# Embedding of a language-model tower on one Trainium2 core: half of the hidden tiles finished by TensorE and ScalarE, and the next stage's first rows loaded one batch earlier

## What is computed

```python
freq, phase, amp = frequencies[ids], phases[ids], amplitudes[ids]          # 64 each
theta = 2 * pi * freq * t[None, :, None] + phase
wave = concatenate([amp * sin(theta), amp * cos(theta)], axis=-1)          # 128 wide
h = einsum('btf,df->btd', wave, W_proj) + b_proj + token_bias[ids]         # 512 wide
h = h + attn(layernorm(h))          # attention reads the normalised rows
h = h + ffn(layernorm(h))           # routed experts and a shared one
```

## Time and profile before

| what | value |
|---|---|
| median of three runs | 3596.42 us |
| the profiled execution's own time | 3624.72 us |
| its span | 3622.9 us |
| embedding, from the start of the span to attention's first matmul | 260.9 us |
| mean granted TensorE clock over the span | 0.943 of full speed |
| busy: PE, DVE, POOL, ACT | 3221.6, 2086.9, 1753.1, 1218.9 us |

### The profile page before, as it was taken

One profiled execution on the slowest core, in us unless ns is written; L12 is line 12 of the kernel. 1 busy time (PEld: TensorE's weight loads), 2 busy tenths in 40 slices (PEclk: granted clock), 3 DMA queues, 4 the chain that ended last, 5 costly groups with the idle time before them and its releaser, 6 DMA issues. The chain is left out here.

```text
span 3622.9 us, 61678 instructions
## 1 busy us (share of the span) xinstructions
PE 3221.6 (89%) x20358; PEld 1667.9 (46%) x20366; DVE 2086.9 (58%) x5798; ACT 1218.9 (34%) x2823; POOL 1753.1 (48%) x988
## 2 busy tenths in 40 slices
PE   4667999989999999999999899999999998687998
PEld 2334444444444444444444444444444444255775
DVE  6843444466646664666466645664566466755555
ACT  3661333333333333333233323332333233311111
POOL 5740354455545553555355535553555355643322
PEclk8878999999999999999999999999999998888999
DMA  5862200121111001010101010101010100205996
GB/s 186 302 255 74 91 30 4 45 73 53 57 69 48 18 16 54 16 36 14 56 16 36 13 54 19 36 13 54 19 36 13 53 19 13 73 4 172 258 254 149
DMA packets 121810, 253.64 MB, mean 70 GB/s; under 512 B 38749, under 2 KB 39389, under 8 KB 118929
## 3 DMA queue, kind: packets, MB, share of 16 engines
q1 hardware_dynamic: 77152, 200.36, 16.4%
q0 software_dynamic: 44048, 49.26, 5.3%
q10 hardware_dynamic: 288, 0.00, 0.0%
HBM read 144.61 MB, written 202.16 MB: 96 GB/s over the span
## 5 line engine op out<-in xcount | busy, mean ns | idle before, releaser
L967 POOL TENSOR_TENSOR a_first_probs<-a_first_probs,a_probs 128x2048 f32<-128x2048 f32 (+3 forms) x320 | 1031.5, 3224 | 1010.8 <-ACT a_probs L1047 928.4
L1205 DVE CUSTOM_DVE_ANT_0 a_unused<-a_ps_ring,a_work 128x512 bf16<-128x512 f32 (+3 forms) x1536 | 779.0, 555 | 897.9 <-PE a_ps_ring L1535 894.0
L1047 ACT ACTIVATE a_probs<-a_ps_ring 128x512 f32<-128x512 f32 (+3 forms) x1280 | 508.2, 473 | 365.0 <-PE a_ps_ring L1569 256.0
L1559 PE MATMUL a_ps_ring<-a_k_t,a_q_t 32*128 32x512 f32 (+3 forms) x3072 | 436.7, 536 | 78.1 <-DVE a_row_max L1205 52.6
L1535 PE MATMUL a_ps_ring<-a_q_t,a_k_t 32*128 32x512 f32 (+3 forms) x3072 | 393.8, 552 | 14.5 <-DVE a_row_max L1205 12.5
L978 POOL DMA_INDIRECT d_slots<-a_rows,a_place_i x349 | 350.0, 1003 | 71.9 <-issue 61.2
L1559 PEld LDWEIGHTS a_ps_ring<-a_k_t,a_q_t 32*128 32x128 f32 x3072 | 156.4, 185 | 281.3 <-issue 130.4
L1535 PEld LDWEIGHTS a_ps_ring<-a_q_t,a_k_t 32*128 32x128 f32 x3072 | 145.2, 190 | 283.4 <-issue 257.4
L974 POOL TENSOR_TENSOR a_attn_t<-a_attn_t,a_sum_inv 128x512 f32<-128x512 f32 x64 | 83.2, 1301 | 379.8 <-DVE a_sum_inv L1220 379.8
L1047 ACT ACTIVATE a_first_probs<-a_ps_ring 128x512 f32<-128x512 f32 x256 | 135.8, 606 | 381.9 <-PE a_ps_ring L1569 356.9
L1582 PE MATMUL a_ps_heads<-a_probs,a_values 128*32 128x512 f32 (+3 forms) x2560 | 261.6, 481 | 0.0
(11 more groups left out here) (283 smaller groups left out, 4325.9 us busy)
## 6 DMA issues: line engine op xcount, KB each, us to landing
d_hidden<-e_hidden SPq DMA_DIRECT2D x8, 2048.0 KB
d_normed_t<-e_normed_t SPq DMA_DIRECT2D x8, 2048.0 KB, 11.8
a_work<-d_normed_t SPq DMA_DIRECT2D x7, 2048.0 KB
a_hidden<-d_hidden SPq DMA_DIRECT2D x56, 256.0 KB, 2.7
out<-a_hidden SPq DMA_DIRECT2D x56, 256.0 KB
d_slots<-a_rows SPq DMA_DIRECT2D x32, 408.8 KB, 5.9
x_rows<-d_slots SPq DMA_DIRECT2D x32, 408.8 KB
x_w_gate<-w_gate SPq DMA_DIRECT2D x16, 512.0 KB
```

The lines of the kernel that those rows point to most:

```text
L967: nc.gpsimd.tensor_tensor(total_of, total_of, probs_of(m)[:, :, 0:width], ALU.add).then_inc(added, 1)
L1047: nc.scalar.activation(probs_of(m)[:, h, 0:width], score_bank(m, h)[:, 0:width], ACT.Exp).then_inc(exp_done, 1)
L1205: nc.vector.tensor_tensor_reduce(unused[:, (HG * k + h) % N_UNUSED, 0:width], row_bank(k, h)[:, 0:width], decay[:, at:at + width], 1.0, NE ...
L1559: nc.tensor.matmul(score_bank(m, h)[:, 0:width], q_t[st.g][dims, j * P:(j + 1) * P], k_t[st.g][dims, i0:i0 + width], start=True, stop=False)
```

## The change

Tiles with odd t are treated in another way. TensorE adds their token bias rows itself, by a third matmul with the identity as weights and the gathered rows as moving operand (f32, 512 columns, L491 of the changed kernel), and ScalarE then moves the finished tile from PSUM to `hidden` (its own `take_hidden`, at L412, placed last in its step of tile t). It counts in a new semaphore `hidden_taken`. Even tiles stay with DVE as they were. Whoever waited for `hidden_done` now waits for the one of the two counters that belongs to the tile, or for both (POOL before it gathers over a buffer, SP before it loads into one).

The load of attention's first rows stands behind batch 5 in SP's order and no longer behind batch 6.

```diff
+        def by_act(t):
+            return t % 2 == 1
+        def wait_hidden(eng, n):
+            if n >= 0:
+                eng.wait_ge(hidden_taken if by_act(n % NT) else hidden_done, n // 2 + 1)
+        def wait_batches(eng, count):
+            eng.wait_ge(hidden_done, NT // 2 * count)
+            eng.wait_ge(hidden_taken, NT // 2 * count)
...
-                if b == NB - 2:
-                    sp.wait_ge(hidden_done, NT * (NB - 2))
+                if b == NB - 3:
+                    wait_batches(sp, NB - 2)
...
             def take_stats(b, t):
-                dve.wait_ge(hidden_done, NT * b + t + 1)
+                wait_hidden(dve, NT * b + t)
...
-                    take_hidden(b, t)
+                    if not by_act(t):
+                        take_hidden(b, t)
...
+            def take_hidden(b, t):
+                if t == 1:
+                    wait_from_1(act, hidden_out[b % 3], 16 * (b // 3))
+                act.wait_ge(hid_ps_full, NT * b + t + 1)
+                nc.scalar.activation(hidden[b % 3][:, t, :], ps_hid[(NT * b + t) % 3][:], ACT.Identity).then_inc(hidden_taken, 1)
...
                             take_turned(b - 1, t - 2)
+                    if b < NB and by_act(t):
+                        take_hidden(b, t)
...
-                wait_from_1(pe, hidden_done, n - 2)
+                wait_hidden(pe, n - 3)
                 nc.tensor.matmul(bank[:], ones_b[:], b_parts[:], start=True, stop=False)
-                nc.tensor.matmul(bank[:], waves_t[b % 2][:, t, :], w_proj[:], start=False, stop=True).then_inc(hid_ps_full, 1)
+                mm = nc.tensor.matmul(bank[:], waves_t[b % 2][:, t, :], w_proj[:], start=False, stop=not by_act(t))
+                if by_act(t):
+                    if t == 1:
+                        pe.wait_ge(rows_in[b % 3], 16 * NT * (b // 3 + 1))
+                    mm = nc.tensor.matmul(bank[:], ident[:], rows[b % 3][:, t, 3 * NF:NROW], start=False, stop=True)
+                mm.then_inc(hid_ps_full, 1)
```

More of the change, by code:

```diff
@@ L194, in embed @@
         normed_out = [sem(f"normed_out{p}") for p in range(2)]
+        hidden_taken = sem("hidden_taken")
         N_CONSTS = 4
         ANGLE_STEPS = 8
+        def by_act(t):
[6 more added lines that the diff above has]
+            eng.wait_ge(hidden_taken, NT // 2 * count)
         block = ctx.enter_context(nc.Block())
@@ L252, in _ @@
                 if 1 <= b < NB - 2:
-                    pool.wait_ge(hidden_done, NT * b)
+                    wait_batches(pool, b)
                 for t in range(NT):
```

## The result

The changed kernel takes **3611.32 us** (median of 7 runs, 3608.91 to 3613.00) against 3596.42 of the kernel before (7 runs): ratio 1.0037, 95% interval 1.0025 to 1.0049. It is 15 us (0.4%) slower. The forecast was 10.8 us faster, with a range of 3577 to 3597.

What follows compares the result with a forecast made beforehand. In the embedding's middle batches DVE was taken to bound the first half, ACT and PE the second. 10.4 + 1.9 - 3.0 + 1.5 = 10.8 us less, from 3596.4 to 3585.6 us, range 3577 to 3597.

Steps and rivals of the forecast that it cites:

- The 3362 us behind that keep their instructions: Behind the embedding: instructions stay the same, so attention's span was to be unchanged within 2 us.
- Middle batches, 10.4 us: Embedding batches 2 to 5: each gains 2.6 us, from a shorter DVE first half, 10.4 us in all.
- The walk: First half of a middle batch: DVE stepped between POOL's additions, reaching the take of tile 4 2.7 us earlier.
- the additions take the gain back: Rival, embedding batches: DVE arrives earlier but always behind an addition, gaining 0.4 us per batch; 3594.8 us, chance 0.15.
- Batches 0, 1, 6, 1.9 us: These embedding batches gain 0.7, 0.5 and 0.7 us, 1.9 us in sum, bounds 0 and 6.
- Batch 7, a loss of 3.0 us: Last embedding batch, bound by ACT: evictions in every second tile cost 3.0 us, bounds 2.0 and 5.
- the closed chain: Batch 7: eviction, centre, scale, transposes and three matmuls follow one another, 4.36 us per pair of tiles, not 3.41.
- The load, 1.5 us: Embedding's end: with the load behind batch 5, batch 7's stores finish sooner, gaining 1.5 us, bounds 0 and 5.2.
- ACT becomes the bound: Rival, embedding: slow PE delays ACT's sines, 1.1 us lost in each of seven batches; 3605.6 us, chance 0.09.
- a change in attention: Behind the embedding: listed as a sign that the forecast is wrong; attention's span was to stay within 2 us.

Runs made afterwards that it cites:

- after: The changed kernel as profiled, with odd tiles by TensorE and ScalarE and the earlier load, against the kernel before: 3611.32 us, ratio 1.0037.
- e5: The changed kernel plus 64 do-nothing semaphore increments at the end of TensorE's list in the embedding: 3591.24 us, ratio 0.9983.
- e2: The changed kernel without its load part, attention's first rows loaded behind batch 6 as before: 3621.01 us, ratio 1.0062.
- e6: The kernel before plus 128 do-nothing semaphore increments at the end of TensorE's list in the embedding: 3619.33 us, ratio 1.0062.
- e1: The kernel before, unchanged, measured and profiled once more: 3598.48 us, ratio 1.000.
- e7: The changed kernel without POOL's additions of attention's output bias in the embedding, POOL only counting: 3585.06 us.
- e8: The kernel before without POOL's additions of attention's output bias in the embedding, POOL only counting: 3570.58 us.
- e13: The changed kernel with 64 increments, POOL's additions moved behind its gathers and out of DVE's first half: 3579.47 us, ratio 0.9943.
- e14: The kernel before with POOL's additions moved behind its gathers and out of DVE's first half: 3580.20 us, ratio 0.9947.
- e3: The kernel before with only the load of attention's first rows moved behind batch 5: 3597.48 us, ratio 1.0002.
- e15: The kernel of e13 with seven of each batch's eight POOL additions also waiting for DVE's last multiplication of the waves: 3574.59 us, ratio 0.9935.
- e16: The kernel before with the same POOL order as e15: 3578.96 us, ratio 0.9946.

## Why the prediction was wrong

**"The 3362 us behind that keep their instructions", so attention's span is unchanged.** This step failed, and it made the sign. The instructions are the same, their place in TensorE's program is not. What the second stall brings with it costs some 13 to 20 us: after and e5, which differ by 64 increments, are 20.1 us apart (3611.32 and 3591.24), of which 1.9 lie in the embedding, and by the profiles the five batches of the loop are 12.6 (after), 15.5 (e2) and 16.3 us (e6) longer than in e1. Shown are the stall, that it depends on the number of instructions ahead of the loop, and that neither the split nor the starting time is needed for it. The queues of after (columns: packets, MB, share) are

```profile
q8 instruction: 170, 2.79, 0.3%
```

so 16 KB per packet. I take q8 for TensorE's program and the stall for a fetch that comes too late for a piece beginning shortly behind the loop's head. The packets at the heads fit this in every trace, to within 0.6 us, but for the two named above; it remains a reading of the traces, since no run changed the fetches themselves.

**Middle batches, 10.4 us.** Failed: 27.4 to 27.9 us against 27.3, a loss of 0.1 to 0.6 each. The walk's first steps were right (L308 ahead of the first addition, L311 behind it, L313 at 0.43). It failed where it let L300 and L302 "fit before the next addition" and put L313 "just ahead of the addition due": an instruction that starts 0.2 to 0.4 us ahead of an addition was taken to win. L302 (L315 of the changed kernel) began 0.37 us ahead as in the walk, and waited 1.5 us; L313 (L326) came 2.6 us later than in the walk, 0.24 ahead of the addition after the one named, and waited 1.4. The profile of the kernel before had the case already: there L300 began 0.10 us ahead of an addition and took 1.67 us, not the 0.4 of the walk:

```profile
114.53 1.67 DVE L300 TENSOR_SCALAR e_turns<-e_theta 128x512 f32<-128x512 f32 x1
```

```profile
114.63 1.27 POOL L238 TENSOR_TENSOR e_hidden<-e_hidden,e_b_out 128x512 f32<-128x512 f32 x1
```

So the case **the additions take the gain back** is nearest to what happened in the middle batches; it had 0.15, and allowed a gain of 0.4 each. e7, e8, e13 and e14 show that the additions beside DVE's first half take the first half's gain. That it would have reached the end of the batch was wrong as well: without the additions 2.0 us in the first half leave 1.3 in the batch.

**The Trainium skill** ("SBUF — State Buffer", section "SBUF: two separate sides"), by which whoever starts first keeps the port pair for one whole instruction, led the walk. That additions hold up DVE's angle instructions agrees with the rows here. That the one with the earlier start wins does not agree with L315 at 112.80, by the starts that the profile gives: in before, e1, after, e2 and e5 all 40 instructions of this kind (TENSOR_SCALAR) that began 0.10 to 0.37 us ahead of an addition waited for its end, while all 18 multiplications (TENSOR_TENSOR) of after, e2 and e5 that began 0.11 ahead got through, and the addition took 1.7 us. Why they differ is not shown. And in e13 an instruction once waited through six additions in a row, where the others met by a run waited for one at most.

**Batches 0, 1, 6, 1.9 us.** Batch 0 gained 1.6 and batch 6 2.5, where 0.7 was put for each; batch 1 lost 0.9, where a gain of 0.5 was put. Sum 3.2, so the sum is near by errors that offset each other. Batch 0 itself takes 18.35 us in after and 16.65 in e2 and e5.

**Batch 7, a loss of 3.0 us.** Right: 18.71 against 15.49, 3.2 us. ACT's period was 1.70 us per tile; from one L412 to the next it is now 4.5 us for two tiles, where the closed chain was put at 4.36:

```profile
222.60 0.60 ACT L412 ACTIVATE e_hidden<-e_ps_hid 128x512 f32<-128x512 f32 x1 [0.49 <-PE e_ps_hid L491]
...
227.10 0.60 ACT L412 ACTIVATE e_hidden<-e_ps_hid 128x512 f32<-128x512 f32 x1 [0.48 <-PE e_ps_hid L491]
```

**The load, 1.5 us.** Right, 1.4 in e3 against e1 and 1.5 in after against e2, from batch 7's tile 0 to the embedding's end.

**ACT becomes the bound**, the slower rival, gave 3605.6 but is not what happened: outside batch 7 ACT still waits for the angles. Its time was near by chance; no case had the loss in attention, and "a change in attention" stood only as a sign of being wrong.

## What to carry to other kernels

When a change adds instructions ahead of a loop, look at the engine's idle time without a cause ("issue") just behind the jump, in both kernels, before anything else is explained; a few do-nothing instructions where the engine waits anyway tell whether the loop's place in the program is at fault, and here gave back 20 us. Before work is taken off VectorE beside a busy GpSimd, count the GpSimd instructions that lie beside it: moving those gave 17 us with the split (e15 against e5) and about 19 without it (e14, by its ratio), the whole change on top of it about 4, which is not clear of the noise (e15 against e16). And one profile can lie 28 us above its kernel's median, so profile the kernel before again before comparing.

## What the runs showed of the hardware

- With 128 TensorE instructions more ahead of a loop, every iteration behind a jump had a second stall of 0.8 to 2.0 us and took 366.8 to 368.9 us, where most took 361.7 to 365.6; with 0, 32, 192 or 256 more there was no second stall.
- The stalls end 1.2 to 1.8 us behind the end of a 16 KB instruction packet (112 of 114).
- The stall has an echo: the clock granted to the 7.4 us behind it was 0.61 to 0.71, and 0.75 to 1.00 without it.
- A semaphore increment on TensorE's queue took 0.15 us. 64 of them were hidden in a wait of 11.4 us at the end of the block; 128 were not, and the embedding ended 6.4 us later (e6).
- A TENSOR_SCALAR on VectorE that began up to 0.37 us ahead of a GpSimd addition waited for its end all the same, 40 times in 40.
- A run of GpSimd additions back to back kept a VectorE instruction out for 7.81 us once; the other instructions that met such a run waited for one addition at most.
